# Three SiLU instructions of ScalarE brought together at one slot of a scan kernel

## The reference

```
xs, res = split(rmsnorm(layernorm(x)) @ W_in)       # 512 + 512 features
xs  = silu(conv4(xs) + conv_b)                      # "SiLU of x"
dt  = softplus(xs @ W_x[:, :512] @ W_dt);  B, C = xs @ W_x[:, 512:]
h_t = exp(A * dt_t) * h_(t-1) + dt_t * B_t * xs_t   # 512 features x 16 states, along the tokens
y   = sum over the states of h_t * C_t
y   = y * silu(res)                                 # "SiLU of the gates"
x   = x + layernorm(layernorm(x) + y @ W_out)
logits = silu(layernorm(x) @ router_w1) @ router_w2 # "SiLU of the router"
...  # softmax over the tokens, top 64 per expert and sequence, 16 experts, combine, layernorm, residual
```

## Time and profile before

| what | value |
|---|---|
| time, median of 3 runs (lowest to highest) | 2185.17 us (2182.62 to 2185.49) |
| span of the profiled execution, first to last instruction | 2180.9 us |
| median less that span | 4.3 us |
| busy share of DVE, POOL, PE, ACT | 86%, 83%, 77%, 65% |
| start of the scans of tile 1, of tile 15 | 233.8 us, 1838.1 us |
| a tile between these, from first scan to first scan of the next | 114.6 us (1604.3 / 14) |

### The profile page before, as it was taken

One profiled execution on the slowest core, in us unless ns is written; L12 is line 12 of the kernel. 1 busy time (PEld: TensorE's weight loads), 2 busy tenths in 40 slices (PEclk: granted clock), 3 DMA queues, 4 the chain that ended last, 5 costly groups with the idle time before them and its releaser, 6 DMA issues. The chain is left out here.

```text
span 2180.9 us, 23218 instructions
## 1 busy us (share of the span) xinstructions
PE 1681.2 (77%) x5620; PEld 648.2 (30%) x5620; DVE 1878.9 (86%) x2070; ACT 1411.6 (65%) x2547; POOL 1810.3 (83%) x770
## 2 busy tenths in 40 slices
PE   7777879887888978788879787978888884651690
PEld 3222323232232323232323232323232231220690
DVE  2477999999999999999999999999999999996221
ACT  2565676867686768777777777776867685531121
POOL 0275999999998989898989999999999998950556
PEclk9897979889898979798979798989889895665795
DMA  2663367676667585757475656667576667427742
GB/s 92 163 181 86 88 136 158 129 159 137 146 146 154 126 175 113 167 114 166 108 159 136 146 137 144 154 136 157 126 151 148 137 139 152 110 73 234 245 106 63
DMA packets 168981, 305.16 MB, mean 140 GB/s; under 512 B 27648, under 2 KB 87810, under 8 KB 168864
## 3 DMA queue, kind: packets, MB, share of 16 engines
q1 hardware_dynamic: 137696, 240.13, 44.6%
q0 software_dynamic: 30784, 62.85, 16.1%
q10 hardware_dynamic: 384, 1.05, 0.2%
HBM read 77.82 MB, written 39.52 MB: 54 GB/s over the span
## 5 line engine op out<-in xcount | busy, mean ns | idle before, releaser
L1022 DVE TENSOR_TENSOR_SCAN room<-pa,carry,room 128x512 f32<-128x512 f32 x1024 | 1243.4, 1263 | 69.8 <-ACT pa L871 56.1
L1221 POOL TENSOR_TENSOR room<-room 128x2048 f32<-128x2048 f32 x256 | 1172.7, 4591 | 144.2 <-ACT carry L864 144.2
L871 ACT ACTIVATE pa<-room,neg_a 128x512 f32<-128x512 f32 x1024 | 695.1, 687 | 352.7 <-DVE room L1022 338.6
L520 PE MATMUL py<-room,blk 128*32 128x512 f32 x2048 | 338.8, 734 | 150.5 <-DVE gate L1028 95.8
L1008 DVE TENSOR_TENSOR room<-room,pb 128x2048 f32<-128x2048 f32 x192 | 434.0, 2260 | 0.8 <-DMA room<-du 0.8
L1214 POOL TENSOR_TENSOR room<-room,b_rep 128x2048 f32<-128x2048 f32 x64 | 290.3, 4536 | 6.5 <-DVE room L1022 4.6
L584 PE MATMUL pp<-xs,w_dtx 128*128 128x512 f32 x512 | 254.0, 631 | 18.0 <-DVE du L951 11.7
L593 PE MATMUL pb<-bc,sel_b 32*128 32x512 f32 x288 | 204.3, 796 | 66.2 <-DVE room L1008 66.2
L548 PE MATMUL pp<-xsp,w_conv 128*128 128x512 f32 x512 | 242.2, 606 | 8.4 <-ACT xsp L738 8.4
L540 PE MATMUL pp<-xnt,w_in 128*128 128x512 f32 x256 | 170.2, 800 | 71.7 <-ACT xs L745 59.4
L520 PEld LDWEIGHTS py<-room,blk 128*32 128x32 f32 x2048 | 44.7, 117 | 347.8 <-issue 222.5
(11 more groups left out here) (185 smaller groups left out, 1860.0 us busy)
## 6 DMA issues: line engine op xcount, KB each, us to landing
room<-du SPq DMA_DIRECT2D x1016, 128.0 KB, 2.4
du<-du POOLq DMA_DIRECT2D x56, 512.0 KB, 6.5
room<-in_L_ffn_w_dram SPq DMA_DIRECT2D x39, 512.0 KB, 7.4
room<-bc_scratch SPq DMA_DIRECT2D x64, 256.0 KB, 5.0
du<-late POOLq DMA_DIRECT2D x28, 512.0 KB, 6.3
combine_scratch<-zeros SPq DMA_DIRECT2D x16, 520.0 KB, 9.7
xt<-in_L_attn_x_dram SPq DMA_DIRECT2D x16, 512.0 KB, 4.4
b_rep<-bc_scratch SPq DMA_DIRECT2D x64, 128.0 KB, 5.4
```

What stands on the lines that cost most here:

```text
L520: mm = pe.matmul(py[32 * j:32 * j + 32, :], blk[:], h[:, quad % 4, j, :], start=(g == 0), stop=(g == 3), tile_position=(0, 32 * j))
L871: act.activation(pa[:, decay_bank(t), :], rep[:, c % 2, t % 4, 0, :], ACT.Exp, scale=neg_a[:, a_column(t):a_column(t) + 1]).then_inc(s_exp, 1)
L1022: v.tensor_tensor_scan(h[:, quad % 4, t % 4, :], pa[:, decay_bank(t), :], bq[:, quad % 2, t % 4, :], carry[:, par, t:t + 1], ALU.mult, ALU ...
L1221: pool.tensor_tensor(h[:, quad % 4], h[:, quad % 4], c_rep[:, par, quad % 4, :].unsqueeze(1).broadcast_to((P, 4, T)), ALU.mult).then_inc(s ...
```

## The change

The SiLU of the gates of every tile, and that of the router, get slot 77 in place of 84: they stand at unit 13 of a step in place of unit 20. Nothing else is changed.

```diff
 PREP = dict(
     ...
-    pe_res=(27, 30, 33, 36), act_res=(29, 32, 35, 38), silu_g=84, keep_r=24,
+    pe_res=(27, 30, 33, 36), act_res=(29, 32, 35, 38), silu_g=77, keep_r=24,
 ...
 POST = dict(
     ...
-    store_hid=59, pe_ht=(60, 63), act_ht=(62, 65), pe_w1=(66, 67), raw=70, silu=84, pe_w2=87,
+    store_hid=59, pe_ht=(60, 63), act_ht=(62, 65), pe_w1=(66, 67), raw=70, silu=77, pe_w2=87,
```

More of the change, by code:

```diff
@@ L64 @@
     ln=((19, 0, 1), (27, 1, 2), (77, 2, DC)), s=(20, 28, 79, 82), o2=(21, 29, 80, 83), o3=(22, 30, 81, 84),
-    u=(23, 31, 82, 85), rep=(24, 40, 84, 95), pe_res=(17, 25, 32, 36), act_res=(24, 29, 36, 42), silu_g=84, keep_r=30)
+    u=(23, 31, 82, 85), rep=(24, 40, 84, 95), pe_res=(17, 25, 32, 36), act_res=(24, 29, 36, 42), silu_g=77, keep_r=30)
 SECOND = dict(
@@ L73 @@
     ln=((36, 0, 1), (48, 1, DC)), s=(38, 50, 53, 56), o2=(39, 51, 54, 57), o3=(40, 52, 55, 58),
-    u=(41, 53, 56, 59), rep=(52, 63, 79, 95), pe_res=(22, 24, 26, 30), act_res=(23, 25, 27, 31), silu_g=84, keep_r=24)
+    u=(41, 53, 56, 59), rep=(52, 63, 79, 95), pe_res=(22, 24, 26, 30), act_res=(23, 25, 27, 31), silu_g=77, keep_r=24)
 FIRST_SLOT = FIRST["pe_turn"][0]
@@ L79 @@
     load=-13, pe_out=(10, 11, 12, 13, 16, 17, 19, 20), dve_z=(15, 22), stats=(24, 42), pow=(27, 49), z2=30, x1=32,
-    store_x1=35, hid=57, store_hid=59, pe_ht=(60, 63), act_ht=(62, 65), pe_w1=(66, 67), raw=70, silu=84, pe_w2=87,
+    store_x1=35, hid=57, store_hid=59, pe_ht=(60, 63), act_ht=(62, 65), pe_w1=(66, 67), raw=70, silu=77, pe_w2=87,
     act_lg=89, store_lg=90)
```

## The result

| | before | changed |
|---|---|---|
| median (lowest to highest, runs) | 2185.33 us (2182.62 to 2188.45, 4) | 2201.14 us (2200.32 to 2204.36, 4) |
| ratio to before, 95% interval | | 1.0073 (1.0059 to 1.0088) |
| span of the profiled execution | 2180.9 us | 2198.9 us |
| first scan of tile 1 to that of tile 15 | 1604.3 us | 1618.2 us |

The change makes the kernel 15.8 us slower in the medians, 18.0 in the spans.

A forecast was written before the change was run, and what follows sets the result against it. DVE, busy 86%, was taken to bound the kernel, with little cover for ACT at unit 16. Terms 14.5 + 0.8 + 2.0 + 2.3 - 0.4 = 19.2 us on 2185.2 gave 2204; range 2188 to 2217 (8 in 10).

The forecast's parts named there:

- The cover: At unit 16, decay 16 ends only 0.34 us (tile 9) or 0.22 us (tile 8) before DVE starts scan 16.
- The lateness: Unit 13's longer ACT group starts decay 16 2.32 us later; scan 16 is 2.19 us late in tile 9, 2.31 in tile 8.
- the eleven tiles taken to be alike: Eleven tiles like 8 and 9, unit 20 starting 1.45 and 1.18 us later there: 14.5 us together.
- The wait at unit 20 as slack: DVE's wait before scan 20 (1.01 us in tile 9, 0.86 in tile 8) is POOL's and absorbs that much delay.
- The loads worth nothing: Removing 29 table loads, 37 us of ACT's time at unit 20, gains 0, being off DVE's path.
- The rule to batch calls by set: Speaks for the faster rival (ACT's time counts, 2149 us, chance 0.09); values the 29 loads at an estimated 77 us.
- The queue behind it: PE's dt product and ACT's Abs slip about 1.5 us; scan 19 stays covered by 0.8 us; cost nothing.
- the rival of the clock: PE idles before the dt product, which then runs at a lower clock: 13 us more, 2217; chance 0.11.
- The delay stays: From unit 25 PE waits for DVE's gated product, so a late unit 20 makes the rest of the tile late.
- swallowed later: Rival: PE paces tile starts, so DVE comes 1.2 us later and waits less at unit 4; 2185 us, chance 0.10.
- what PE does behind such a wait moves along: Against swallowing: PE waits for DVE some two times a tile, so its later work, projection included, shifts too.
- Tile 0: Step 0: 3.2 us added ahead of unit 16, the wait of 3.55 at unit 23 goes: -0.4 us.

The follow-up runs named there:

- the Identity in the changed kernel: Changed kernel with an added Identity over the gates (128 x 2048, 1.81 us, values unchanged) at unit 13: 2247.85 us, ratio 1.0284.
- router alone: Kernel before with only the router's SiLU moved to slot 77, the gates' SiLU staying at 84: 2183.56 us, ratio 0.9998.
- Identity at unit 20: Kernel before with Identity in place of the gates' and the router's SiLU at unit 20, so no table load there: 2179.41 us, ratio 0.9974.
- early `u`: POOL's products u of the second pair at slots 56 and 57, not 60 and 61: kernel before 2181.51 us (0.9979), changed kernel 2198.56 us (1.0051).
- another order: Changed kernel with the gates' SiLU behind that of x at unit 13, then the router's; same loads: 2212.43 us, ratio 1.0131.
- `FIRST` as before: Changed kernel with tile 0's gates' SiLU back at slot 84: 2201.49 us, ratio 1.0071.
- the loads put back: Changed kernel with a small SiLU (128 x 4) added at slot 84, bringing the pair of table loads back to unit 20: 2203.04 us, ratio 1.0089.

## Why the prediction was right, and where its sum was off

**The cover.** Right: 0.34 and 0.22 us were all there was. The shortest proof is the Identity in the kernel before: 1.8 us more on ACT at this place, all else as it was, and the kernel is slower by 11.0 us.

**The lateness.** Right to a few hundredths: 6.84 us from load to decay 16 as worked, a wait of 2.16 where 2.19 was worked out for tile 9, 2.34 for 2.31 in tile 8. But these two wait longest among the eleven tiles taken to be alike: on average scan 16 waits 2.09 there and not 2.25, and their term came to 12.2 and not 14.5.

**The wait at unit 20 as slack.** Right: all 11.9 us of it went. The name in the profile's bracket was ACT in tile 9; the row of POOL that ended 0.13 us before the scan was the better witness, and in tiles 3, 5, 6, 7 and 12 of the kernel before the bracket names POOL for the same wait. That POOL holds the whole of it is too much said: in tile 8 its inputs end 0.49 before the scan, and 0.34 can stay there when POOL is early. The delay took that up as well.

**The loads worth nothing.** Right for tiles 1 to 14 (0.6 us for the 14 pairs that the Identity took out); not quite for tile 0, where they gave 2.7; in the changed kernel, where they were put back, up to 7 us of 36 stay possible. The rule to batch calls by set (the Trainium skill, ScalarE: Activation LUTs, Table sets: the hidden batching unit) does what it says to ACT, 34.6 us less work here, but the time went up by 15.8: what ACT saves in sum is no gain here, where DVE waits for one instruction of ACT's list.

**The queue behind it.** Right in the size that mattered: PE idles 1.52 us before the product (1.5 worked out), the Abs comes 2.03 behind decay 16's start (2.76 before), and no wait arises at units 17 to 19, save in tile 1. There the product ran in part at the lower clock (the window over it has a granted clock of 0.69), after an idle time hardly longer than in tile 9 (1.52):

```profile
263.22 5.40 PE L584 MATMUL pp<-xs,w_dtx 128*128 128x512 f32 x8 [1.55 <-ACT xs L753]
```

```profile
263.20:268.70 5.50, 5.48 (x10) 0.69 0.94 211
```

Tile 1 took 2.0 us more in place of 0.8, 1.51 of it the wait at unit 19. This is the rival of the clock, in 1 tile of 14. The run with the Identity in the changed kernel shows that it was near: with PE idle for 3.35 it comes in 11 tiles.

**The delay stays, mostly.** For tiles 1 to 14 I worked out 19.6; 13.9 came. The new waits, 29.5, less the 11.9 at unit 20 are 17.6, so the terms by tile were 2.0 too large; another 4.0 came off the waits at the tiles' starts, units 0 to 7. This sum is 29.9 to 32.0 in the kernel before and the runs that leave unit 16 nearly as it was (router alone, Identity at unit 20, early `u`) and 26.9 to 27.1 in the change and three of its variants (another order, early `u`, `FIRST` as before), but 33.2 with the loads put back and 33.6 with the Identity added to the change, so the 4.0 is likely and not certain. It would be the rival "swallowed later", at a seventh of the size of the new waits (4.0 of 29.5). The step that it touches is "what PE does behind such a wait moves along, the projection too": on these rows that holds for most of a tile's delay, not for all of it.

**Tile 0.** Mis-sized: -0.4 worked out, +3.6 measured. The step failed where the wait at unit 23 was taken as the end of it. I counted what stands behind the SiLU for DVE, and not the instructions for PE in the same list, which made PE idle and then slow (3.78 for 1.98), and the delay came back at unit 27. In the run with the loads put back PE idled as long, ran the second piece in 1.98, and the wait at unit 27 was as before the change: about half of the 3.6, then, hangs on when PE's clock comes back. With this entry undone tile 0 is 3.3 shorter and the kernel no faster, so what the term is worth at the end stays open.

The time came out at 2201 where 2204 was forecast, in part by luck: the two errors, 4.0 too little in tile 0 and 5.7 too much in tiles 1 to 14, partly cancel. 19.2 was worked out; it is 18.0 in the spans and 15.8 in the medians.

## What to carry to other kernels

Ask of each instruction on a side engine which one behind it the critical engine waits for first, and how much cover is there; work moved ahead of that one cost its full length beyond the cover here, less what a later wait took up, however much the engine's sum shrank. Where a wait stands a little further on, find whose it truly is by the row that ends just before it: if it belongs to a third engine, it takes up a delay of its own size and no more. And follow a moved instruction to every engine that its queue feeds, at the first pass of the loop too, where the list holds other things.

## What was not expected of the hardware

The same three SiLU in another order cost 11 us more, nearly all of it where DVE waits behind a slow PE: 5.0 to 6.5 us for eight 128 x 512 matmuls, in place of 3.7, in 11 of 14 second dt products, after PE idled longer ahead of the logits (2.0 to 2.6 us in tiles 2 to 14, 1.2 in the changed kernel). An idle time doesn't decide it by its length: in the changed kernel 1.60 us (tile 2) were followed by 3.69 and 1.55 (tile 1) by 5.40, and with the Identity added to it 3.43 us were followed by 3.69 in tile 10 and by 5.39 in tile 8. What of PE's work before it does decide it, these runs leave open.
